# Scores of a graph attention layer as 64-row fp32 products on TensorE's row halves

## The reference, cut to what matters

```python
q = (x @ Wq + bq).reshape(b, m, h, d); k = ...; v = ...          # d = 64, h = 8
scores = einsum('bmhd,bnhd->bhmn', q, k) * scale + edge_bias[edges]
attn = softmax(where(edges > 0, leaky_relu(scores, 0.2), -1e9), axis=-1)
out = einsum('bhmn,bnhd->bmhd', attn, v).reshape(b, m, h * d) @ Wp + bp
```

## Time and profile before

| | |
|---|---|
| runs, us | 9004.63, 9005.03, 9019.0; median 9005.03 |
| profiled execution: span, us | 9019.7 (no other time of this execution is listed) |
| mean granted TensorE clock | 0.959 |
| busy: TensorE, VectorE, ScalarE, GpSimd | 90%, 82%, 78%, 16% |
| TensorE L670, q_hi and q_lo | 2048 + 2048 matmuls, 852.2 + 655.5 us busy |
| TensorE L666, mask | 2048 matmuls, 636.7 us busy |
| VectorE L1205, q_low | 128, 156.3 us busy |
| ScalarE L908, q copy | 128, 130.7 us busy |
| SyncE L381 | 22% of the chain that ended last |

### The profile page before, as it was taken

The page is one execution under the profiler, slowest core; times in us unless marked ns, Lnnn a source line. Parts: engine busy times, 40 slices in busy tenths (PEclk is TensorE's granted clock), DMA queues, the critical chain, the costliest instruction groups (busy, mean ns, idle before and its releaser), DMA issues.

```text
span 9019.7 us, 165963 instructions
## 1 busy us (share of the span) xinstructions
PE 8145.7 (90%) x58360; PEld 3645.7 (40%) x58360; DVE 7407.4 (82%) x11189; ACT 7012.7 (78%) x8204; POOL 1428.7 (16%) x582
## 2 busy tenths in 40 slices
PE   3899998989999999998999989999899998989999
PEld 1534435344353433434334353443534435343352
DVE  3788787988879878798787978878788787988878
ACT  2787786977869778797787878778687786977877
POOL 0301203021030301203012030120302103021000
PEclk7999999999999999999999999999999999999999
DMA  2714426253262623526245271442615426253251
GB/s 73 159 35 107 107 52 156 42 124 87 61 143 51 141 63 71 135 48 157 44 91 122 43 171 36 103 109 54 156 39 115 98 52 152 46 129 77 60 123 19
DMA packets 2150362, 822.71 MB, mean 91 GB/s; under 512 B 1146914, under 2 KB 2129954, under 8 KB 2147362
## 3 DMA queue, kind: packets, MB, share of 16 engines
q1 hardware_dynamic: 2149410, 810.76, 40.5%
HBM read 76.25 MB, written 4.19 MB: 9 GB/s over the span
## 4 chain that ended last, share of the span: by engine, by line
PE 38%; SPq 23%; DVE 15%; issue 13%; ACT 9%; DMA 1%; DVEq 0%; POOL 0%; ACTq 0%; POOLq 0%
SPq L381 22%; PE psum L817 21%; DVE work L1400 6%; ACT work L1043 5%; PE psum L528 3%; PE psum L600 3%; PE psum L695 2%; DVE work L1279 2%; PE psum L670 1%; DVE work L1251 1%; PE psum L523 1%; PE psum L545 1%; ACT spare L886 1%; ACT spare L881 1%; PE psum L784 1%
## 5 line engine op out<-in xcount | busy, mean ns | idle before, releaser
L817 PE MATMUL psum<-work,pick 128*32 128x512 f32 x32768 | 3766.7, 599 | 192.1 <-DVE work L1400 161.5
L1043 ACT ACTIVATE work<-spare,ucol 128x1024 f32<-128x1024 f32 x3402 | 3631.8, 1145 | 51.9 <-PE psum L817 47.3
L1400 DVE TENSOR_SCALAR work<-spare,ucol 128x1024 f32<-128x1024 f32 x4790 | 3248.9, 744 | 72.3 <-PE psum L817 55.9
L817 PEld LDWEIGHTS psum<-work,pick 128*32 128x32 f32 x32768 | 977.8, 110 | 2531.4 <-issue 2069.1
L953 ACT ACTIVATE work<-psum,beta 128x1024 f32<-128x1024 f32 x1024 | 1139.6, 1113 | 559.8 <-PE psum L670 398.5
L1251 DVE CUSTOM_DVE_ANT_0 work<-psum,work 128x1024 f32<-128x1024 f32 x1024 | 1227.0, 1198 | 247.1 <-ACT work L953 237.4
L1279 DVE STREAM_TRANSPOSE work<-work 128x1024 f32<-128x1024 f32 x960 | 1190.9, 1240 | 263.3 <-DMA work<-work 168.7
L960 ACT ACTIVATE work<-work,least 128x1024 f32<-128x1024 f32 x1024 | 1172.7, 1145 | 27.5 <-DVE least L1251 27.5
L1481 POOL TENSOR_TENSOR rstd<-rstd,neg_half 128x8 f32<-128x8 f32 x64 | 131.6, 2056 | 5024.0 <-DVE rstd L1190 5024.0
L670 PE MATMUL psum<-x_split,q_hi 128*128 128x512 f32 x2048 | 852.2, 497 | 0.0
L666 PE MATMUL psum<-mask,ident_b 128*128 128x512 bf16 x2048 | 636.7, 393 | 228.3 <-DVE least L1251 225.1
(11 more groups left out here) (167 smaller groups left out, 7053.2 us busy)
## 6 DMA issues: line engine op xcount, KB each, us to landing
work<-work SPq DMA_DIRECT2D x2560, 128.0 KB, 2.4
spare<-work SPq DMA_DIRECT2D x1280, 128.0 KB, 2.5
adj_in<-in_adj SPq DMA_DIRECT2D x128, 512.0 KB, 4.8
q_lo<-adj_in SPq DMA_DIRECT2D x1024, 64.0 KB, 2.1
q_lo<-spare SPq DMA_DIRECT2D x1024, 64.0 KB, 2.1
work<-work SPq DMA_DIRECT2D x1792, 32.0 KB, 1.9
mask<-mask_next SPq DMA_DIRECT2D x16, 2048.0 KB, 9.2
x_in<-in_x SPq DMA_DIRECT2D x16, 256.0 KB, 10.2
```

Source lines behind the costliest of these rows:

```text
L817: mm = pe.matmul(slot[32 * q:32 * q + 32, cols], pick[:, 15 - kk:47 - kk], ring[kk % 4][q][:, cols], start=False, stop=(kk == 15), skip_gr ...
L1043: ins = act.activation(ring[kk % 4][q], v3, ACT.Relu, bias=ucol[:, 4 * T + q, kk:kk + 1])
L1400: ins = dve.tensor_scalar(ring[kk % 4][q], v3, ucol[:, 4 * T + q, kk:kk + 1], 0.0, ALU.add, ALU.max)
```

## The change

The score operands are kept in fp32 and are no longer split. `x_two` and `q_two` hold x and q twice on the partitions, as the products deliver them. For each half c of 512 columns the product uses partitions 64c to 64c + 63 of both, so the first half goes to the upper 64 rows of the array and the second to the lower ones, each writing a PSUM bank of its own. VectorE's subtractions are gone; ScalarE's copy frees the slot. The borrowed buffers get memory of their own.

```diff
-HIS_A = 5
-HIS = H - 2 + 1
+HIS_A = 2
+HIS = 1
...
-        x_split = sb("x_split", [P, N], F32R)
-        q_hi = sb("q_hi", [P, 2, 2, N], F32R)
-        q_lo = sb("q_lo", [P, 2, 2, N], F32R)
+        x_two = sb("x_two", [P, N])
+        q_two = sb("q_two", [P, 2, 2, N])
+        moved_pair = sb("moved_pair", [P, 2 * N])
+        columns = sb("columns", [P, 2, N], F32R)
...
-                for k, left in enumerate((q_hi[:, pair % 2, h, rows_], q_lo[:, pair % 2, h, rows_])):
-                    for c in range(2):
-                        cols = slice(c * HALF, (c + 1) * HALF)
-                        mm = pe.matmul(slot[:, cols], left, x_split[:, cols], start=False, stop=(k == 1))
+                for c in range(2):
+                    half = slice(c * F, (c + 1) * F)
+                    cols = slice(c * HALF, (c + 1) * HALF)
+                    mm = pe.matmul(slot[:, cols], q_two[half, pair % 2, h, rows_], x_two[half, cols], start=False,
+                                   stop=True)
                 mm.then_inc(s_scores, 1)
...
-                    act.activation(x_split[:], turn, ACT.Copy).then_inc(s_hi_a, 1)
-
-            def q_high(it, h, count):
+                    act.activation(x_two[:], turn, ACT.Copy).then_inc(s_turn_free, 1)
+
+            def q_copy(it, h):
                 filled(act, it, ("q", h))
-                act.activation(q_hi[:, h // 2 % 2, h % 2, :], turn, ACT.Copy).then_inc(count, 1)
+                act.activation(q_two[:, h // 2 % 2, h % 2, :], turn, ACT.Copy).then_inc(s_turn_free, 1)
...
-            def q_low(it, h, g):
-                if h < 2:
-                    dve.wait_ge(s_hi_a, g * HIS_A + 3 + h + 1)
-                else:
-                    dve.wait_ge(s_hi, g * HIS + h - 1)
-                dve.tensor_tensor(q_lo[:, h // 2 % 2, h % 2, :], turn, q_hi[:, h // 2 % 2, h % 2, :].bitcast(F32),
-                                  ALU.subtract).then_inc(s_turn_free, 1)
...
-                if u == SPAN + 56:
-                    dve.wait_ge(s_hi_a, g * HIS_A + 3)
-                    dve.tensor_tensor(x_split[F:P, :], turn[F:P, :], x_split[F:P, :].bitcast(F32), ALU.subtract)\
-                       .then_inc(s_turn_free, 1)
-                if u == SPAN + 60:
-                    q_low(it, 0, g)
-                if u == SPAN + 64:
-                    q_low(it, 1, g)
...
-                    if extra and extra[0] == "q":
-                        q_low(it, extra[1], g)
```

More of the change, by code:

```diff
@@ L238, in build @@
         tile3T = work[:, 5, :]
-        column3 = q_hi[:, 0, 0, :]
-        columnA = q_hi[:, 0, 1, :]
+        column3 = columns[:, 0, :]
+        columnA = columns[:, 1, :]
         heads3 = [yout[:].rearrange("p t f -> p (t f)"), heads_T[:, HALF:N]]
         blocksA = [adj_in[:].rearrange("p a b -> p (a b)").bitcast(F32), spare[:, 0:2 * N]]
-        pairA_T = q_lo[:, 1, :, :].rearrange("p a b -> p (a b)").bitcast(F32)
+        pairA_T = moved_pair[:]
         s_load = sem("s_load")
@@ L934, in ahead @@
                         act.wait_ge(s_ring_free, ONE + g * GROUPS - 11)
-                    q_high(it, 0, s_hi_a)
+                    q_copy(it, 0)
                 if u == SPAN + 60:
@@ L940, in ahead @@
                 if u == SPAN + 63:
-                    q_high(it, 1, s_hi_a)
+                    q_copy(it, 1)
             def relu(g, n):
@@ L984, in layer2 @@
                     if extra and extra[0] == "q":
-                        q_high(it, extra[1], s_hi)
+                        q_copy(it, extra[1])
                     if extra and extra[0] == "vw":
```

## The result

The changed kernel takes 9050.16 us (median of 8 runs) against 9008.75 of the kernel before (8 runs on the same chip): ratio 1.004, 95% interval 1.003 to 1.005, so it is slower by 41 us. The profiled execution spans 9050.7, 31.0 more than the one before. The forecast was 9023.

The account below looks back on a forecast made before the run. Layer 2 was taken as bound by the DMA-issuing queue, except its opening, where it waits for compute. Per graph 1.03 - 0.69 + 0.77 + 0.1 = 1.2; over 15 graphs +18 us on 9005.03 gives 9023, range 8975 to 9110.

Parts of the forecast that it names:

- The passes side by side: Layer 2 scores on TensorE: the two 64-row halves overlap in full, 2 x 0.43 a tile.
- both rivals without full overlap: Layer 2 scores: no overlap, 1.00 more a tile, about 9665 (6%); half overlap, 0.57 more, about 9268 (6%).
- A tile, 1.51: TensorE, layer 2: mask 0.45, switch 0.10, weight load 0.10, passes 2 x 0.43; 0.14 more than now.
- 0.10 again where a product on the whole array follows: TensorE, layer 2: switching back after a tile's scores costs a further 0.10 before a whole-array product.
- The estimate with a drain of 0.17: TensorE: with the isolated 166 ns pipe constant, each switch costs 0.07 more, the sum some 27 us higher.
- Late blocks, +0.77 and +0.1: Layer 2 after the third move: six-tile chains 1.14 longer make two blocks a graph late, by 0.77 and 0.1.
- Within 0.5 us of 150 to 152: Sign of being right: the queue's third to fifteenth move stay within this time a graph.
- a hole over 1 us: Sign of being wrong: the DMA-issuing queue shows such holes in layer 2 from the third move on.
- The head, -0.69: End of layer 3: without the last subtraction the exponential starts 0.69 earlier a graph, limited by the value copy.
- The opening, +1.03: Layer 3's end to the third move: four tiles' longer scores, two at the lower clock, add 1.03 a graph.
- the faster rival: Opening: the clock stays at its upper level, saving 5.8 a graph, about 8935; chance 8%.
- Dearer switches: Layer 2 scores: the halves' weights load one after the other, 0.1 to 0.2 more a tile, 9050 to 9077; 15%.

Follow-up runs that it names:

- e2_one_half: The changed kernel with both column halves on the same 64-row half, so no passes can lie side by side: 9811.29 us, ratio 1.0896.
- e4_row_mask: The changed kernel with the mask re-laid out and its product on row halves too, VectorE's untaken branch longer, small buffers packed: 9031.79 us, ratio 1.0025.
- e1_rounded: The changed kernel with the old four rounded 128-row passes back, low parts left out, still no VectorE subtractions: 8994.38 us, ratio 0.9988.
- e9: The kernel before with the next graph's loads (x, two adjacency tiles) issued after the second move, not at layer 3's end: 9007.67 us, ratio 0.9994.

## Why the prediction was right or wrong

The time lies in the range, and at the upper edge of the forecast's own 8998 to 9050; the loss is 41 where 18 were forecast. The direction and the mechanism were right. A tile's price was too small, and one of the late blocks was looked for at the wrong move, so the two parts do not nearly cancel: the products cost 47 to 54, and the subtractions give 11 to 16 back.

- **The passes side by side: right.** The second pair's two passes are a x2 in the narrow stretch, e2_one_half shows that 0.85 a tile are hidden, and both rivals without full overlap fall. The Trainium skill ("TensorE: Matmul & The Clock Gate", Part 3, The mechanism) has matmuls start and end in program order, which made 9268 if each half's two passes stand together; here two passes start together at 1945.27, and as passes on one half follow each other (e2_one_half), they are of both halves.
- **A tile, 1.51: too small, and this is the step that failed.** "0.10 again where a product on the whole array follows" was booked for the q and value products alone (three in the chain of six, two a block, one in the opening). But the next tile's mask goes over the whole array too. So each tile pays the change of division twice, 0.08 in and 0.09 back, and ahead of a mask, a q product or the value product of the next pair it grows by 0.22, not by 0.14. Only ahead of a product of a moved block with the values was 0.14 right (0.13), as the way to column halves cost 0.09 before as well; the sum's 4.62 for a step left that out. The Trainium skill ("TensorEngine Tiling (Array Packing)", Key Properties) says that a change of mode drains the engine; the trace agrees, twice a tile, and e4_row_mask, where nothing changes within a tile, is without it. The estimate with a drain of 0.17 gave a sum 27 higher, 9050; that this is the measured time is luck, since a change costs 0.08 to 0.09 here.
- **Late blocks, +0.77 and +0.1: too small, by the same term and by a second step that failed.** The chain of six tiles grew by 1.57, forecast 1.14. At the first place the pauses grew by 1.01 in all (seventh and eighth moves), forecast 0.77. At the second an adjacency load was said to stand between; it does stand ahead of the twelfth move, and there 0.16 came of the forecast 0.1. But the chain of six ends a block earlier, at the eleventh move, which has no load ahead of it and only 0.54 to spare on the mean, and which the sum left out: 1.30. The moves from the third on take 2.12 more a graph, not 0.87. "Within 0.5 us of 150 to 152" was wrong, already for the kernel before (152.72 on the mean, where graph 3 has 150.46), and the prediction's own sign of being wrong, a hole over 1 us, came.
- **The sum once more.** With 0.09 more a tile, and two of the 0.10 in a chain instead of three, the forecast's own sum becomes 1.03 + 0.54 - 0.69 + 0.77 + 0.44 + 0.1 + 0.44 = 2.63 a graph, 39 in 15. That it meets the 41 measured is partly luck: the second part is 1.75 in it and 2.12 in the traces, head and first two moves are +0.88 in it and -0.16 in the traces, and the two profiled executions differ by 31.0 only.
- **The head, -0.69: right in size, not in its account.** The exponential came 0.78 earlier on the mean, limited by the value copy as said, and e1_rounded shows 12.7 in all against the sum's 10. But "the branch is over by 1889.2" took its 6.43 as a fixed time after the last instruction. e9 shows that it is none: with the loads moved away the gap is at most 4.20. The maximum in the changed kernel was in time because the wait began 4.5 earlier, not because a branch takes 6.4.
- **The opening, +1.03: near.** Head and first two moves together changed by -0.16, forecast +0.34, with the clock unchanged, so the faster rival had nothing to stand on. The graphs scatter there by some 1.5 (standard deviation), so that half a microsecond is not settled.
- **Dearer switches, the rival at 9050 to 9077:** its time came true, its cause did not. The weights of the halves load side by side (four loads in 0.30); it is the change back that costs.
- **Hidden, as said:** subtractions in the second part (e1: 152.66 against 152.72 of the moves), copies and the moved buffers.

## What to carry to other kernels

Count changes of the array's division in both directions and for every product between two others: here two pairs side by side (0.86) were shorter than four rounded passes (0.92), but with a whole-array product between any two tiles they brought 0.28 of changes and bare weight loads with them. An engine that is a little under the bounding queue on average can still be the bound at the places where its extra products fall, so price the longest chain, not the mean, and check for each late block what really stands ahead of it in the queue. Idle time marked "issue" behind a branch is not a constant: look at what the DMAs carry at that moment before counting on it or against it.

## What the runs showed of the hardware

- The code behind a branch competes with data transfers: the same branch cost 6.43 with the DMA engines 53% busy, no more than 4.20 at 3%, and with them 95% busy the second instruction stood 2.71 behind the first, over 12 after the branch. The code's own DMA packet started 3.65 behind the last instruction in the first case and 0.84 behind it in the second.
- Weight loads are placed ahead while passes of the same division run (pairs 0.43 apart in e4_row_mask), and are not across a change of it (0.54 in the changed kernel).
- A change of the array's division costs 0.08 to 0.09 each way: from the whole array to row halves and back, and from the whole array to column halves (a tile of the kernel before takes 1.37 ahead of a mask, 1.46 ahead of a moved block's product).
